# One kernel of twelve sections on two interleaved streams: a shorter lead of one stream, a two-part attention shift, and a loop body of two passes

## The reference

```
L0_delta  gated delta rule with short convolutions      L2_attn   16 heads, rotary, causal
L0_cross  16 heads of 8, keys and values from a context L2_cross  16 heads, given mask
L0_ffn    gated, width 384                              L2_moe    14 experts, top 1
L1_attn   16 heads, causal                              L3_mamba  selective scan over 128 tokens
L1_mix    linear mix with the context's mean            L3_cross  4 heads of 32, rotary, padding mask
L1_moe    8 experts, top 2, and a shared one            L3_moe    8 experts, capacity 512, top 1
```

```python
w = jnp.einsum('bhnd,bhmd->bhnm', q, k) * jax.lax.rsqrt(float(D))
w = jnp.where(mask > 0, w, NEG)
w = jax.nn.softmax(w, axis=-1)
attn = jnp.einsum('bhnm,bhmd->bhnd', w, v)
```

## Time and profile before

| | |
|---|---|
| median of three runs | 4269.26 us (4267.58 to 4272.39) |
| the profiled execution | 4276.39 us |
| its span, first to last instruction | 4274.6 us |
| busy: PE, DVE, ACT, POOL | 3953.5, 3100.6, 1978.4, 662.4 us |
| granted TensorE clock, mean | 0.947 of full speed |

### The profile page before, as it was taken

How to read it: one execution, slowest core, us unless ns; L and a number is a source line. 1 busy time by engine, 2 the same in 40 slices (tenths; PEclk the granted TensorE clock), 3 DMA queues, 4 the chain that set the end, 5 groups by cost and what they waited for, 6 DMA issues and landing times. The chain is left out here.

```text
span 4274.6 us, 102265 instructions
## 1 busy us (share of the span) xinstructions
PE 3953.5 (92%) x41486; PEld 2859.7 (67%) x41486; DVE 3100.6 (73%) x8220; ACT 1978.4 (46%) x4830; POOL 662.4 (15%) x988
## 2 busy tenths in 40 slices
PE   4899999999999999999999999999999999999998
PEld 3576676766667666666667667676666766666675
DVE  5568787686876868678676886768777687875782
ACT  2355453544536444364534546354453535436551
POOL 2110202111120110201112020110202112020003
PEclk6899999998999999999999999999999999989999
DMA  3300000000000000000000000000000000000003
GB/s 92 75 2 1 9 1 9 2 9 2 1 10 1 9 2 1 10 1 9 2 9 2 1 9 1 9 2 1 9 1 10 2 8 2 1 9 1 1 1 103
DMA packets 52842, 46.20 MB, mean 11 GB/s; under 512 B 8354, under 2 KB 48914, under 8 KB 52126
## 3 DMA queue, kind: packets, MB, share of 16 engines
q1 hardware_dynamic: 48076, 32.94, 2.8%
q0 software_dynamic: 2560, 5.79, 0.4%
q10 hardware_dynamic: 1714, 0.63, 0.1%
HBM read 27.25 MB, written 12.62 MB: 9 GB/s over the span
## 5 line engine op out<-in xcount | busy, mean ns | idle before, releaser
L2447 PE MATMUL banks<-ident_bf 128*128 128x256 bf16 x5310 | 877.0, 277 | 37.8 <-issue 32.9
L2447 PEld LDWEIGHTS banks<-ident_bf 128*128 128x128 bf16 x5310 | 512.3, 100 | 230.8 <-issue 120.7
L876 ACT ACTIVATE scratch<-banks 128x512 f32<-128x512 f32 x512 | 280.1, 598 | 178.4 <-PE banks L800 177.5
L766 PE MATMUL banks<-scratch 32*128 32x512 f32 x2048 | 343.2, 657 | 10.0 <-DVE scratch L925 3.6
L912 DVE TENSOR_REDUCE scratch<-banks 128x4 f32<-128x512 f32 x512 | 323.1, 678 | 14.4 <-PE banks L736 5.4
L341 ACT ACT_TABLE_LOAD x249 | 319.5, 1283 | 27.4 <-PE banks L1093 23.3
L1749 DVE TENSOR_TENSOR_SCAN scratch<-scratch 128x512 f32<-128x512 f32 x256 | 312.7, 1222 | 9.9 <-ACT scratch L1692 4.1
L1692 ACT ACTIVATE scratch<-scratch,ssm_A 128x256 f32<-128x256 f32 x512 | 229.9, 503 | 159.0 <-DVE scratch L1749 157.5
L1604 PE MATMUL banks<-scratch,w_ident 128*128 128x256 f32 x1024 | 271.6, 387 | 19.6 <-DVE scratch L1755 19.6
L589 POOL TENSOR_TENSOR 0_rstd<-0_var,minus_half 128x2 f32<-128x2 f32 x96 | 74.2, 773 | 1294.7 <-DVE 0_var L607 1095.7
L1890 PE MATMUL banks<-scratch 32*32 32x32 f32 x10496 | 247.9, 209 | 27.8 <-issue 22.8
(11 more groups left out here) (524 smaller groups left out, 8224.2 us busy)
## 6 DMA issues: line engine op xcount, KB each, us to landing
expert_in<-scratch SPq DMA_DIRECT2D x1, 4112.0 KB, 27.5
experts<-in_e_W SPq DMA_DIRECT2D x14, 256.0 KB
scratch<-expert_in SPq DMA_DIRECT2D x2, 1542.0 KB, 12.2
w_e_W<-in_e_W SPq DMA_DIRECT2D x3, 704.0 KB
experts<-in_e_w SPq DMA_DIRECT2D x1, 1792.0 KB, 8.5
experts<-in_e_w SPq DMA_DIRECT2D x2, 896.0 KB, 12.6
scratch<-expert_in SPq DMA_DIRECT2D x2, 514.0 KB, 4.1
1_xres<-in_x SPq DMA_DIRECT2D x8, 128.0 KB, 2.2
```

The costliest lines, as they stand in the source:

```text
L766: last = pe.matmul(row_tiles(t), lhs[r, col(s)], rhs[r, s], start=True, stop=letter == "S" and mask is None, skip_group_check=True)
L876: P.give(act.activation(pT[:, s % 2, j, :], t, ACT.Exp), f"{nm}.T{s}{j}")
L2447: pe.matmul(banks[:, bank, 0:N].rearrange("p (s f) -> p s f", s=G), ident_bf[:], spread(ident_bf[:], G), start=True, stop=True, skip_group ...
```

## The change

Four things are changed together.

1. Stream 1 leads by four sections, not six: it begins a pass with L1_mix. "first" has four sections of stream 1 (L0_delta to L1_attn), the last pass has eight of it.
2. The loop takes two passes in each of its three turns, and the eighth pass stands in one stretch with the last one. Within a stretch nothing is cleared between passes: semaphore counts run on (before(name) adds those of the passes before) and a bank's name gets the pass as a tag (PassBanks). Five barriers are left of nine.
3. The shift has two parts, not three: the upper halves of the f32 words of the negated maximum, read in place as bf16, and the upper halves of what is left after taking them off. One DVE instruction takes the place of four. Four matmuls turn the parts, one for each 32 rows of mT, and the 16 selecting matmuls take 32 rows each (K = 32), i outside and j inside, so that neighbours use different rows of the array and different banks. The mask comes behind them. The shift thus has about 16 bits. ACT copies v into vslot with one instruction per sequence, not four, and POOL's clearing of mparts is gone.
4. All strings of turns are new. Fillers: 671 in a pass of the loop and 613 in the last before (5,310 in the run); 1,532 in two passes and 1,725 in the last two now (6,321 in the run).

```diff
-ROUND = [SECTIONS[k:] + SECTIONS[:k] for k in (0, 6)]
+ROUND = [SECTIONS[k:] + SECTIONS[:k] for k in (0, 4)]
...
-    c["sel_part"] = ((i[:, :1] % 32 == np.arange(NH)[None, :]) & (i[:, :1] < 96)).astype(np.float32)
+    c["sel_part"] = (i[:, :1] % 16 == np.arange(NH)[None, :]).astype(np.float32)
...
-                    negm, mrest = (S.take(G * NH).rearrange("p (s h) -> p s h", s=G) for _ in range(2))
-                    mparts = S.take(N, BF16).rearrange("p (s f) -> p s f", s=G)
+                        shift_flat = S.take(G * 2 * NH)
+                        negm = shift_flat.rearrange("p (s k h) -> p s k h", s=G, k=2)[:, :, 0, :]
+                        mparts = shift_flat.bitcast(BF16).rearrange("p (s a w) -> p s a w", s=G, w=2)[:, :, :, 1]
...
-                            P.close(pe.transpose(t.bitcast(BF16)[:, 0:L], mparts[:, s, :], ident_bf[:]), f"{nm}.mT{s}")
+                                for j in range(NJ):
+                                    last = pe.matmul(t[32 * j:32 * j + 32, 0:L], mparts[:, s, :], ident_bf[:], start=True,
+                                                     stop=True)
+                                P.close(last, f"{nm}.mT{s}")
...
                             products(s, "T", qk[1], qz)
-                            for j in range(NJ):
-                                if j % 2 == 0 and j:
+                                yield
+                                P.wait_given(pe, f"{nm}.mT{s}")
+                                for i in range(NI):
+                                    for j in range(NJ):
...
-                                    last = pe.matmul(t[:, i * L:(i + 1) * L],
-                                                     sel_part[:, a:a + 1].broadcast_to([128, 128]), mT[:, col(s)],
-                                                     start=False, stop=i == NI - 1, skip_group_check=True)
+                                        r = slice(32 * j, 32 * j + 32)
+                                        last = pe.matmul(P.bank(f"{nm}.T{s}{j}")[:, i * L:(i + 1) * L],
+                                                         sel_part[r, a:a + 1].broadcast_to([32, 128]), mT[r, col(s)],
+                                                         start=False, stop=mask is None and i == NI - 1, skip_group_check=True)
...
-                            m, r = negm[:, s, :], mrest[:, s, :]
-                            q.link(dve.tensor_copy(mparts[:, s, 0:NH], m))
-                            q.link(dve.tensor_tensor(r, m, mparts[:, s, 0:NH], ALU.subtract))
-                            q.link(dve.tensor_copy(mparts[:, s, 32:32 + NH], r))
-                            dve.tensor_tensor(mparts[:, s, 64:64 + NH], r, mparts[:, s, 32:32 + NH],
+                                dve.tensor_tensor(mparts[:, s, NH:2 * NH], negm[:, s], mparts[:, s, 0:NH],
                                               ALU.subtract).then_inc(ev(f"{u}.mparts"), 1)
...
-        with nc.Fori(0, NGROUPS - 1) as g:
-            stretch("round", g)
-        stretch("last", NGROUPS - 1)
+        with nc.Fori(0, NGROUPS - 2, 2) as g:
+            stretch(["round", "round"], g)
+        stretch(["round", "last"], NGROUPS - 2)
```

More of the change, by code:

```diff
@@ L80 @@
[L80 to L90, removed]
@@ L2031, in act_f @@
+                            for s in range(G):
+                                yield
+                                t = P.take(act, f"{nm}.X5{s}")
+                                for q in (quads[0], quads[2]):
+                                    last = act.copy(TT64[q, s, :, 32:64], t[q].rearrange("p (h t) -> p h t", h=DELTA_H))
+                                P.give(last, f"{nm}.X5{s}")
                             yield
@@ L2056, in act_f @@
+                            act.activation(msq[:, 0, :], mixed, ACT.Square).then_inc(ev(nm + ".msq"), 1)
                             yield
[L2057 to L2059 removed]
+                            act.wait_ge(ev(nm + ".weighted"), 1 + before(nm + ".weighted"))
+                            act.activation(msq[:, 1, :], mweighted, ACT.Square).then_inc(ev(nm + ".msq"), 1)
@@ L2336, in program @@
-                start = ROUND[u].index("L0_delta") if FIRST[u] else len(SECTIONS)
-                order = {"first": ROUND[u][start:], "round": ROUND[u], "last": ROUND[u][:start]}[part]
-                sections = {name: makers[name]() for name in order}
-                at_v = TURN[u]
-                x_d, c_d, m_d = (a.rearrange("(g u s) t f -> u g t s f", u=STREAMS, s=G)[at_v]
-                                 for a in (dram["x"], dram["ctx"], dram["mask"]))
-                r_d = out.rearrange("(g u s) t f -> u g t s f", u=STREAMS, s=G)[at_v]
@@ new lines, in one @@
+                    start = ROUND[u].index("L0_delta") if FIRST[u] else len(SECTIONS)
+                    order = {"first": ROUND[u][start:], "round": ROUND[u], "last": ROUND[u][:start]}[part]
+                    sections = {name: makers[name]() for name in order}
+                    at_v = TURN[u]
+                    x_d, c_d, m_d = (a.rearrange("(g u s) t f -> u g t s f", u=STREAMS, s=G)[at_v]
+                                     for a in (dram["x"], dram["ctx"], dram["mask"]))
+                    r_d = out.rearrange("(g u s) t f -> u g t s f", u=STREAMS, s=G)[at_v]
@@ new lines, in one @@
+                    context = {0: ctx_pe, 1: ctx_act, 2: ctx_dve, 3: ctx_pool}
+                    return load, steps
+                ones = [one(turn, part) for turn, part in enumerate(passes)]
+                def steps(engine, *args):
+                    for turn, (_, run) in enumerate(ones):
+                        yield from run(engine, *args)
+                def landed(sp):
+                    sp.wait_ge(s_in, 16 * total)
+                    sp.wait_ge(s_ctx, 48 * total)
+                return ones[0][0], landed, steps, [s_in, s_out, s_ctx]
@@ L2464, in turn_sems, with stretch @@
                     list(events.values()))
-        def stretch(part, g):
+        def stretch(passes, g):
             P = Psum(banks, filled, emptied)
-            turns = {"first": [""] * 5, "round": TURNS, "last": LAST_TURNS}[part]
+            first, last = passes[0] == "first", passes[-1] == "last"
+            turns = [""] * 5 if first else END_TURNS if last else TURNS
             tables.now = None
-            groups = [make(P, part) for make in streams]
+            groups = [make(P, passes) for make in streams]
             with nc.Block() as block:
@@ L2501, in _ @@
                     in_turns(turns[4], P, groups, 4, sp, g)
-                    if part != "last":
+                    if not (last and len(passes) == 1):
                         for _, landed, _, _ in groups:
                             landed(sp)
-                    if part == "first":
+                    if first:
                         sp.wait_ge(s_zero, 16)
```

3370 lines of the change are left out of this document (1722 added, 1648 removed).

## The result

The changed kernel takes 4248.77 us (median of 5 runs, 4239.71 to 4259.68), the kernel before 4272.39 on the same chip (4267.58 to 4287.38). The ratio is 0.9949, 95% interval 0.9931 to 0.9967: 0.5% faster, about 22 us, where 94 were forecast.

What follows compares the result with a forecast made beforehand. DVE bounds some windows, elsewhere chains of waiting steps do. From 4276.4 us profiled, -37.3 - 2 + 21 - 26 - 64 + 12 = -96 gives 4180; runs' median 7 lower, so 4175 us, range 4085 to 4268.

Steps and rivals of the forecast that it cites:

- Lead of four, "first": The opening stretch loses stream 1's L1_mix and L1_moe, which stood alone there: -37.3 us.
- Lead of four, the last pass: Stream 1 does eight sections beside stream 0's twelve; 418 us becomes 439: +21, bounds +2 and +43.
- The barriers: Four of nine barriers between passes go, 6.5 us each: -26 us, bounds -10 and -33.
- The shift: Attention: less DVE and PE work, 8 us a pass in eight passes, -64 (bounds -32, -172); -2 in "first".
- less about 4 for the shift: Deduction within the last pass's forecast: 443 us less about 4 gives 439.
- The new turns: 1,011 more fillers on PE, some too many ahead of norms: +12 us, 1.5 a pass, bounds 0 and +110.
- What is late next in an attention is ACT's exponentials: In an attention, after the shift's savings, ACT's exponentials were named as the next late step; no size given.
- Rival (a): DVE bounds more of a pass, savings show nearly whole and the clock rises: 4090 us; chance 0.21.
- Rival (b): No change: PE's slots give the true planned time, so passes stay about as long: 4271 us; chance 0.12.
- Rival (c): Slower: fillers stand before ready work on PE: 4288 us; chance 0.09.
- (d): PE's selections don't pack, 16 take 0.88 us, exponentials begin later: 4225 us; shares the main forecast's 0.58.

Runs made afterwards that it cites:

- run 1: Kernel before with the new attention shift alone (lead of six, old turns, nine barriers): 4214.14 us, ratio 0.9869 to the kernel before.
- run 2: Changed kernel with a barrier after each pass again, the turns of a pass as they are: 4268.01 us, ratio 0.9994 to the kernel before.
- run 7: Changed kernel with ACT's order alone changed at one place of seven full passes (L0_cross beside L2_moe), exponentials grouped: 4170.66 us, ratio 0.9732.
- run 9: run 7 with an expert's second Gelu also moved ahead of the exponentials, and the last pass treated alike: 4169.6 us, ratio 0.9766.
- run 4: Changed kernel with three more small DVE instructions at each of 160 places and the selecting matmuls ordered bank by bank: 4269.34 us, ratio 1.0007.
- run 11: run 7 with three more small DVE instructions at 160 places and the selecting matmuls over all 128 rows: 4247.61 us, ratio 0.9942.
- runs 5, 6 and 12: Changed kernel with filler rows halved (ratio 0.9943), with no fillers in loop and last two passes (1.002); run 7 with filler rows halved (0.9776).
- run 8: run 7 with eight loads of ACT's function table put back in each pass, the grouped order kept: 4254.15 us, ratio 0.9955.

## Why the prediction was wrong

The sign was right (faster, held at 0.83) and the time lies inside the range, but a quarter of the forecast gain came. The spans take the miss apart: the shift alone -60 (run 1), the lead and the new turns together +53 (run 2 over run 1), four barriers -21 (the changed kernel under run 2), in all -28. The prediction had -66, -4 and -26. By its own terms:

- **Lead of four, "first", -37.3:** the first norm of stream 0 comes at 156.92 and not 193.84, -36.9. Right.
- **Lead of four, the last pass, +21:** the last pass is 460.7 us in run 2 and 427.8 in run 1, +33. The tail from L2_cross, forecast 155, is 149 to the store and about 154 to the end: right. The part ahead of it is 296 us where 284 were worked out, and this is the 12 that were missing. Why is open. L0_cross takes 51.4 there too, where the full passes of run 7 have 39.9, but not for the same reason: PE waits only 2.4 us for ACT in it, at a clock of 1.00, and run 9 moved 3 us of it. The lead by itself brings about 4 us and not 16.
- **The barriers, -26:** 24 in the old turns, 19 in the new (21 by the spans). Right, a little over-sized. PE's gap of 5.3 us at a barrier is still there at 1169.79, and there is none of that kind at the seam (PE busy 3.6 of 5 us from 658).
- **The shift, -64 and -2:** 55 by the medians of run 1, 60 by the spans, 8.1 a pass. Right. The sum counted the last pass twice, once in the eight passes and once in "less about 4 for the shift"; run 1 gives it 3. In the changed kernel DVE's part is worth 25 (run 4); on the cleared turns both parts are worth 90 (run 11).
- **The new turns, +12:** this is the step that failed: "I count +12 for such places, 1.5 a pass; bounds 0 and +110". Runs 1 and 2 differ by 7.9 a pass, 56 in seven. The size lies in the bounds, but the step asked the wrong engine. It counted the fillers in PE's string and found 0.37 us; runs 5, 6 and 12 show that taking fillers out gives nothing back. ACT's string, which decides how often the function table changes beside an exponential, was not read, and the cost of those changes stood in no term. "What is late next in an attention is ACT's exponentials" was written in the paragraph before, and was so; the step from there to what stands between them was missing.

Rival (a) fell with run 1: the shift showed 8 of its 21.5 us a pass. Rival (b)'s price, 4271, was nearer to the time than the forecast is, but its reason (PE's slots tell the planned time) fell with run 7: same slots, 4171. Rival (c) fell with runs 5, 6 and 12, (d) is refuted by the 0.33 us.

That the loads are the cause is shown by taking them out (run 7) and putting them back (run 8). Of run 7's 12.5 us a pass, seven loads explain 9. In L0_cross, 11 us shorter, PE's wait for L979 gives 8; the rest goes with the clock (0.90 over the section, 1.00 in run 7) or with the order, and was not taken apart.

## What to carry to other kernels

When an order is written anew, read it for every engine, and for ACT as a sequence of function tables: each change is 1.28 us here, and it costs nothing in one place and its whole length between activations that the bound engine waits for. Price a saving in the turns in which it will run: the shift was worth 8.1 us a pass in the old turns and 11.3 in the cleared new ones. A mean busy share (ACT 47%) tells nothing of a 29-us stretch in which the engine is full.

## What the runs showed that was not expected

Matmuls on different row groups of the array overlap even when they aren't written next to each other. In the program of run 4 four selections in a row use the same 32 rows, then the next four the next 32; 16 take 0.36 us, almost as in the interleaved order (0.33), and not the 0.90 of full-height ones.

The clock can fall in a stretch where PE was never idle. Two passes of the changed kernel do the same work ahead of the same place (PE busy 19.9 of 20 us both times, clock 1.00), and then one keeps the full clock (2.4 GHz) over 15 us and the other is mostly at 1.2 GHz:

```profile
520.00:530.00 10.00, 9.89 (x145) 8.64 (x143) 4.10 (x16) 6.71 (x22) 0.00 (x0) 1.00 0.01 2
530.00:545.00 15.00, 15.00 (x100) 10.70 (x98) 9.79 (x31) 9.41 (x21) 0.82 (x2) 1.00 0.00 1
```

```profile
1021.80:1031.80 10.00, 9.89 (x139) 8.59 (x139) 4.10 (x16) 6.80 (x23) 0.00 (x0) 1.00 0.01 2
1031.80:1046.80 15.00, 15.00 (x71) 11.85 (x71) 8.15 (x27) 4.98 (x12) 0.82 (x2) 0.55 0.00 1
```

Stream 0's L3_mamba, which begins there, takes 87.9 us in the first case and 96.0 in the second. Such falls are part of why passes take 502 to 520 us here; the kernel before has 508 to 515. What decides it stays open.
